# Six working slots in place of four for the context tiles of a decoder layer, and the context loop written out on every engine

## What is computed

```python
Kn = _layernorm(K, ln1_g, ln1_b)          # K = V = context, 1601 rows
kn = _l2norm(split_heads(Kn @ wk))        # 16 heads of 64
attn = einsum('bhqd,bhkd->bhqk', qn, kn)
out = einsum('bhqk,bhkd->bhqd', attn, split_heads(Vn @ wv))
x = Q + out @ wo + bo                     # = Q + qn @ M, M made from kn^T Kn, wv and wo
```

## Time and profile before

| | |
|---|---|
| median of 3 runs | 3989.25 us |
| the profiled execution's own time | 3996.92 us |
| its span | 3994.9 us |
| TensorE, matmuls | 2886.1 us busy, 72% |
| VectorE | 2129.4 us, 53% |
| ScalarE | 1274.4 us, 32% |
| GpSimd | 1424.0 us, 36% |
| mean granted TensorE clock | 0.876 of full |
| queue of the data DMAs, share of 16 engines | 26.8% |

### The profile page before, as it was taken

The page is one execution under the profiler, slowest core; times in us unless marked ns, Lnnn a source line. Parts: engine busy times, 40 slices in busy tenths (PEclk is TensorE's granted clock), DMA queues, the critical chain, the costliest instruction groups (busy, mean ns, idle before and its releaser), DMA issues.

```text
span 3994.9 us, 51537 instructions
## 1 busy us (share of the span) xinstructions
PE 2886.1 (72%) x14500; PEld 1878.1 (47%) x14500; DVE 2129.4 (53%) x4209; ACT 1274.4 (32%) x2421; POOL 1424.0 (36%) x860
## 2 busy tenths in 40 slices
PE   0577777777777676777777777777777777677776
PEld 0355544555445444455444554445444455445444
DVE  6536555374643737446373564636555374643736
ACT  1216322172222712236122441215322162221711
POOL 2226222362223622244233532326322362223622
PEclk9979888898788987889878988889888898888987
DMA  6325103340043400443013520316103340043400
GB/s 183 29 47 121 29 6 42 50 126 14 7 47 55 128 6 12 47 76 98 6 17 46 94 75 6 27 38 118 48 6 35 56 126 14 7 47 54 124 11 6
DMA packets 413254, 208.03 MB, mean 52 GB/s; under 512 B 210734, under 2 KB 411078, under 8 KB 412102
## 3 DMA queue, kind: packets, MB, share of 16 engines
q1 hardware_dynamic: 413046, 205.49, 26.8%
HBM read 118.11 MB, written 87.33 MB: 51 GB/s over the span
## 4 chain that ended last, share of the span: by engine, by line
PE 44%; DVE 30%; issue 10%; POOL 4%; DMA 4%; ACT 3%; DVEq 2%; SPq 0%; ACTq 0%; POOLq 0%
PE PS L1278 38%; PE PS L1281 5%; DMA arena<-in_ctx 4%; DVE arena L1072 3%; DVE ss L1063 3%; DVE arena L1113 2%; DVE arena L411 2%; DVE arena L1121 2%; DVE arena L1128 2%; DVE arena L416 2%; DVE arena L408 2%; POOL rn L356 1%; POOL arena L428 1%; POOL rstd L356 1%; DVE bnst L1020 1%
## 5 line engine op out<-in xcount | busy, mean ns | idle before, releaser
L1281 PE MATMUL PS<-ident,arena 128*128 128x128 f32 (+1 forms) x3356 | 584.4, 309 | 729.6 <-POOL arena L428 292.6
L1278 PE MATMUL PS<-arena 128*16 128x128 f32 (+3 forms) x6272 | 809.3, 346 | 153.4 <-DVE arena L1121 74.8
L1281 PEld LDWEIGHTS PS<-ident,arena 128*128 128x128 f32 (+1 forms) x3356 | 417.1, 156 | 954.1 <-POOL arena L428 315.5
L1278 PEld LDWEIGHTS PS<-arena 128*16 128x16 f32 (+3 forms) x6272 | 551.0, 138 | 359.8 <-issue 118.3
L356 POOL TENSOR_TENSOR rstd<-rstd,mhalf 128x1 f32<-128x1 f32 (+3 forms) x153 | 104.2, 681 | 1301.9 <-DVE rstd L1025 697.1
L356 POOL TENSOR_TENSOR rn<-rn,mhalf 128x16 f32<-128x16 f32 (+1 forms) x136 | 413.4, 3040 | 410.8 <-DVE rn L1218 208.3
L694 POOL TENSOR_TENSOR arena<-right_mask,edge 128x1536 f32 (+1 forms) x128 | 368.4, 2878 | 164.2 <-DVE nmax L1113 161.4
L861 ACT ACTIVATE arena<-arena,nmax 128x512 f32<-128x512 f32 x512 | 366.6, 716 | 122.1 <-DVE nmax L1113 111.3
L1278 PE MATMUL PS<-cwk,arena 128*128 128x512 f32 (+1 forms) x832 | 376.3, 595 | 22.0 <-ACT arena L800 19.3
L1113 DVE CUSTOM_DVE_ANT_0 arena<-PS,arena 128x512 f32<-128x512 f32 x512 | 330.0, 684 | 64.8 <-PE PS L1278 62.0
L1020 DVE BATCH_NORM_STATS2 bnst<-arena 128x6 f32<-128x256 f32 (+1 forms) x104 | 44.2, 425 | 546.6 <-DMA arena<-in_ctx 545.6
(11 more groups left out here) (161 smaller groups left out, 4069.6 us busy)
## 6 DMA issues: line engine op xcount, KB each, us to landing
arena<-bias_scr SPq DMA_DIRECT2D x128, 336.0 KB, 3.3
prob_scr<-arena SPq DMA_DIRECT2D x128, 336.0 KB, 2.7
q_scr<-arena SPq DMA_DIRECT2D x128, 128.0 KB
arena<-k_scr SPq DMA_DIRECT2D x64, 256.0 KB, 10.7
arena<-q_scr SPq DMA_DIRECT2D x128, 128.0 KB, 3.1
arena<-in_ctx SPq DMA_DIRECT2D x96, 128.0 KB, 2.1
bias_scr<-arena SPq DMA_DIRECT2D x32, 320.0 KB, 13.6
arena<-prob_scr SPq DMA_DIRECT2D x128, 80.0 KB, 2.3
```

The lines of the kernel that those rows point to most:

```text
L1278: return pe.matmul(o, l, r, start=start, stop=stop, **kw)
L1281: return pe.transpose(o, i, ident[0:i.shape[0], 0:i.shape[0]])
```

## The change

`Kn` gets six slots of 256 columns (`CSLOTS`). It now begins at `only_attn + 1024`, right behind `xnT`, and ends where it ended before. Tile i lies in slot i mod 6 and has the semaphore of that slot. Six tiles are loaded ahead, and the load of tile i+6 stands where that of tile i+4 stood. The buffers that go by tile modulo 4 or 2 (`kns`, `bnst`, `mv`, `rstd`, `cnT`) are as before. Since a body of four turns doesn't fit six slots, `ctx_tiles` is gone and the four engines have all 13 turns written out.

```diff
+CSLOTS = 6
-        Kn = carve(1024, (4, E), only_attn + 1536)
+        Kn = carve(CSLOTS * E, (CSLOTS, E), only_attn + 1024)
-        ctx_loaded = [sem(f"ctx_loaded{q}") for q in range(4)]
+        ctx_loaded = [sem(f"ctx_loaded{q}") for q in range(CSLOTS)]
-                def load_ctx(i, q):
-                    n = crows(i)
-                    sp.wait_ge(cg_done, cdone(b, i - 4) + 1)
+                def load_ctx(i):
+                    n, q = crows(i), i % CSLOTS
+                    sp.wait_ge(cg_done, cdone(b, max(i - CSLOTS, -1)) + 1)
-                for q in range(4):
-                    load_ctx(q, q)
+                for i in range(CSLOTS):
+                    load_ctx(i)
-                    if exists(i + 4):
-                        load_ctx(i + 4, q)
+                    if exists(i + CSLOTS):
+                        load_ctx(i + CSLOTS)
-                ctx_tiles(dve, ctx_dve)
+                ctx_unrolled(ctx_dve)
-                    per = (CT + 3 - q) // 4
-                    dve.wait_ge(ctx_loaded[q], 16 * per * b + 4 * (i - q) + 17)
+                    per = (CT + CSLOTS - 1 - q) // CSLOTS
+                    dve.wait_ge(ctx_loaded[q], 16 * (per * b + i // CSLOTS + 1) + 1)
-                    x = Kn[0:n, q, :]
+                    x = Kn[0:n, i % CSLOTS, :]
```

More of the change, by code:

```diff
@@ L447, in ctx_unrolled @@
                 body(i, i % 4)
-        def ctx_tiles(eng, body):
-            with eng.Fori(0, CMAIN // 4) as it:
-                for q in range(4):
[L454 to L458, removed]
         POOL_EDGES = 3
@@ L678, in ctx_pool @@
                         norm_root(i + 1, q + 1)
-                ctx_tiles(pool, ctx_pool)
+                ctx_unrolled(ctx_pool)
                 pool.wait_ge(cg_done, cdone(b, CT - 1) + 1)
@@ L825, in ctx_act @@
                         square(i + 2, (q + 2) % 4)
-                ctx_tiles(act, ctx_act)
+                ctx_unrolled(ctx_act)
                 act.wait_ge(cg_done, cdone(b, CT - 1) + 1)
@@ L1014, in norm_stats @@
                 def norm_stats(i, q):
-                    n, p = crows(i), q % 2
+                    n, p, q = crows(i), q % 2, i % CSLOTS
                     st = Steps(dve_norm, "dve_norm", b * CT + i)
-                    per = (CT + 3 - q) // 4
-                    dve.wait_ge(ctx_loaded[q], 16 * per * b + 4 * (i - q) + 17)
+                    per = (CT + CSLOTS - 1 - q) // CSLOTS
+                    dve.wait_ge(ctx_loaded[q], 16 * (per * b + i // CSLOTS + 1) + 1)
                     st(dve.bn_stats(bnst[0:n, p, :], Kn[0:n, q, :]))
@@ L1345, in t_ctx @@
                     for c in range(2):
-                        ins = tr(bank(6 + p, c * 128, c * 128 + n), Kn[0:n, q, c * 128:(c + 1) * 128])
+                        ins = tr(bank(6 + p, c * 128, c * 128 + n), Kn[0:n, i % CSLOTS, c * 128:(c + 1) * 128])
                     ins.then_inc(ct_psum, cinc(i))
@@ L1361, in g_ctx @@
                     for m in range(NM):
-                        ins = mm(bank(m // 2, (m % 2) * E, (m % 2 + 1) * E), kns[0:n, q, m * 128:(m + 1) * 128], Kn[0:n, q, :],
+                        ins = mm(bank(m // 2, (m % 2) * E, (m % 2 + 1) * E), kns[0:n, q, m * 128:(m + 1) * 128], Kn[0:n, i % CSLOTS, :],
                                  False, True, skip_group_check=True)
@@ L1382, in ctx_pe @@
                     g_ctx(i, q)
-                ctx_tiles(pe, ctx_pe)
+                ctx_unrolled(ctx_pe)
                 pe.wait_ge(g_act, 2 * (b + 1) + 1)
```

## The result

The changed kernel takes 3636.28 us, median of 4 runs (3634.22 to 3642.68), beside 3994.38 us for the kernel before on the same chips (4 runs). The ratio is 0.9105, 95% interval 0.9081 to 0.9129: 358 us or 9.0% faster. That range had been given a chance of 0.80.

The account below looks back on a forecast made before the run. Waits for context loads were taken to bound the kernel, with TensorE's 7.64 us turn next. The stage falls from 129.9 to 88.8 us, 41.1 us in each of 8 batch elements: 329 us, from 3989.25 to 3660 us, range 3642 to 3712.

Parts of the forecast that it names:

- That range: The author's own range for the changed kernel's time, 3645 to 3690 us, from turns of 7.5 to about 8.0 us.
- What bounds the kernel, and what six slots change: Context stage: a circle of load, VectorE's turn and `g_ctx`, with 545.6 us of load waits; six slots remove wait and circle.
- Rival 4: Context loads still arrive late because stores stand ahead in SyncE's order; the time stays at 3989 us; chance 0.03.
- Writing out the loop costs and brings nothing: Context loop: removing one taken branch per engine and batch element, between turns 3 and 4, brings nothing.
- TensorE is late next, and paces: Context loop without load waits: TensorE's own work sets the turn at 7.64 us; VectorE is early by 2 us.
- The turn of 7.64 us: One TensorE turn in the context loop: 3.56 us `g_ctx` to `k_ctx`, 3.64 to the transposes, 0.44 for two transposes.
- The lower bound of 7.5 us: Shortest turn allowed for TensorE in the context loop, with the modelled ends of the three groups left out.
- Rival 5: The dense context loop misses the high clock: turn 15.3 us, stage 157.7 us, time 4212 us; chance 0.03.
- Rival 3: Stores or reloads become the wait at the stage's end; 10 us late per batch element gives 3740 us; chance 0.04.
- The sum: Context stage after the change: 3.56 us, nine turns of 68.8 us and a tail of 16.45 us, together 88.8 us.
- From the span to the median: Whole kernel: the profiled execution lies 7.7 us above the median, so a 3666 us span goes with a 3660 us median.
- Rival 1: VectorE, held up by GpSimd's root, paces the context loop: turn 8.6 us, 260 us saved, 3729 us; chance 0.08.

Follow-up runs that it names:

- half of `g_ctx`: Every second of the 8 matmuls of `g_ctx` left out, against the changed kernel with six slots; 3519.66 us, ratio 0.8755 to the kernel before.
- the changed kernel's second trace: The changed kernel run again without an edit, on the chip of three later experiments; 3635.32 us, ratio 0.9041 to the kernel before.

## Why the prediction was right in its mechanism and wrong in its size

- **What bounds the kernel, and what six slots change**: right. The waits are gone, the stage's circle with them, and five slots do the same. Rival 4, loads that still come late, falls.
- **Writing out the loop costs and brings nothing**: right, ratio 1.0024 with four slots. The prediction's sentence that the removed branches "would bring something more" took their targets to lie outside the instructions already fetched; nothing here shows where they lay.
- **TensorE is late next, and paces**: right. VectorE's chain was given 2 us of room. `scale_k` ends at 626.72 and `g_ctx` starts at 627.99, so it is 1.3 us, and one more reduction of 1.25 us uses it up. The chain itself was sized rightly: it ends 5.8 us after the start of the `g_ctx` before, where the prediction had 5.7. The room is smaller because TensorE's turn is shorter.
- **The turn of 7.64 us**: this is the step that failed. Measured are 7.11 us: 3.46 + 3.43 + 0.22, where the prediction had 3.56 + 3.64 + 0.44. All three terms were read off rows next to a wait. The 3.64 us from `k_ctx` to the transposes held about 0.1 us of waiting for `norm_apply`, which ends 0.06 us before the transposes start, and 0.1 us because `k_ctx` itself had waited; the pair 780.91 and 784.34 of the earlier trace rows, `k_ctx(12)` and the `g_ctx` behind it, gave 3.43 us and stood in the prediction's own rows. The 3.56 us from `g_ctx` to `k_ctx` held the group's first weight load. In the changed kernel's trace it starts 0.11 us ahead of the first matmul in a dense turn, but together with it after a wait (both at 613.67), and the group is 0.10 us longer; half of `g_ctx` shows the same, 1.83 against 1.73 us. And the 0.44 us for two transposes were their whole duration up to the modelled end, where the next group starts 0.22 us after their start. Nine turns too long by 0.53 us are 4.8 us per stage, 38 us in all.
- **The lower bound of 7.5 us** was thus no bound: it took off 0.14 us of the 0.53 us by which the three terms were too long. By the prediction's own sum it gives 3650 us; the range began a little below, at 3642, and a turn of 7.11 us would have given 3622.
- **Head and tail, 20.0 us**: right; 83.9 - 9 x 7.11 = 19.9 us.
- **The stage before, 129.9 us**: right, 1039.9 / 8 = 130.0.
- **The high clock in a dense loop**: right, 1.00 over 83 us. Rival 5 falls.
- **Reloads covered**: right, with 20 us of room. Rival 3 falls.
- **The sum**: 88.8 against 83.9 us per stage makes the span 39 us too long. The rest of the span grew by 6.7 us, which the prediction had at zero; no one place accounts for it. 4 us of it lie ahead of the stages, 2 right behind them and 2 further on, less 1 before the first, and the changed kernel's second trace had 2958.3. Together they are, but for rounding, the 33.5 us between the 3666 us forecast for this span and the 3632.5 measured.
- **From the span to the median**: luck, in part. The prediction took the profiled execution to be 7.7 us above the median, as before; it was 2.0 us below it. So 9.7 us of the turn's error don't show in the time, and a miss of 33.5 us in the span is one of 24 in the median.
- **Rival 1**, VectorE held up by GpSimd's root: falls. `norm_apply`'s second half and `scale_k` keep 0.48 and 1.22 us in the new rhythm, and the turns are not longer but shorter than forecast.

## What to carry to other kernels

Where a load waits for its slot and the engine for the load, count how many turns earlier the slot comes free with one more: here one was enough and two brought the same. When the next bound is an engine's own work, take its time from start to start between groups that did not wait, and look for such a pair in the tail, where the pipeline drains; the terms read beside a wait were too long here by 0.10 to 0.22 us each, and a loop multiplies them. And a pause of TensorE in a chain can have two prices, the pause and the slow matmuls behind it.

## What the runs showed of the hardware that I had not expected

TensorE work of no use made the kernel with four slots 3% faster (4026 to 3887 us). The granted clock was 1.00 over 115 us of the stage, against 0.86 before. How long a pause was did not by itself decide the clock behind it: in the kernel before, 72 `g_ctx` stood behind pauses of 2.0 to 2.4 us and 0.4 to 0.8 us, 57 of them took 5.1 to 6.8 us and 15 took 3.7. In one stage of the kernel with three more reductions, pauses of 1.47 and 0.70 us were followed by 5.23 us and by 3.72 us. And behind the stage, pauses of 1.57 and 0.88 us were followed by 1.94 and 3.81 us in one kernel and by 3.14 and 5.41 us in another whose tail was just as dense, and by either in different batch elements of the same kernel. So two kernels that differ in the order of a few matmuls differed by 13 to 25 us in stretches that neither edit touches, and a gain of 0.3% in one stage can be hidden by that.
